# Image/text attention: tasks of each turn and of the first preparation from a written table, turned queries copied by ACT and DVE

## The reference, cut to what matters

```python
q = rms_norm(linear(x, q_w, q_b), norm_q_w).reshape(B, L, NH, HD)
k = rms_norm(linear(ctx_txt, k_w, k_b), norm_k_w).reshape(B, -1, NH, HD)       # 1344 text rows
v = linear(ctx_txt, v_w, v_b).reshape(B, -1, NH, HD)
k_img = rms_norm(linear(ctx_img, k_img_w, k_img_b), norm_k_img_w)...           # 257 image rows
v_img = linear(ctx_img, v_img_w, v_img_b)...
out = (attention(q, k, v) + attention(q, k_img, v_img)).reshape(B, L, DIM)     # two softmaxes
x = x + linear(out, o_w, o_b)                                                  # x was layer-normed first
```

## Time and profile before

| what | us |
|---|---|
| runs, median of 3 | 4134.57 (4131.62 to 4142.93) |
| profiled execution | 4128.62, span 4126.9 |
| PE busy in the span | 3621.0 (88%) |
| DVE busy | 2364.4 (57%) |
| ACT busy | 2263.6 (55%) |
| POOL busy | 784.5 (19%) |

### The profile page before, as it was taken

The page is one execution under the profiler, slowest core; times in us unless marked ns, Lnnn a source line. Parts: engine busy times, 40 slices in busy tenths (PEclk is TensorE's granted clock), DMA queues, the critical chain, the costliest instruction groups (busy, mean ns, idle before and its releaser), DMA issues. The chain is left out here.

```text
span 4126.9 us, 64041 instructions
## 1 busy us (share of the span) xinstructions
PE 3621.0 (88%) x23965; PEld 3060.3 (74%) x23965; DVE 2364.4 (57%) x4251; ACT 2263.6 (55%) x5239; POOL 784.5 (19%) x1026
## 2 busy tenths in 40 slices
PE   6756948999999999995888888785999999999977
PEld 5646937888888888885555555474899999998866
DVE  8964746676676676654555555333455555555445
ACT  3314735676666666663455555412666666666622
POOL 0002123222222222211021020001323232222100
PEclk7767978999999999997899999787999999999989
DMA  4114520010010010001000000112010010100001
GB/s 143 64 39 176 204 97 24 19 46 26 19 51 21 19 51 22 9 6 67 33 18 16 33 1 1 41 66 89 22 53 19 27 53 24 53 24 11 11 31 36
DMA packets 54028, 181.93 MB, mean 44 GB/s; under 512 B 5916, under 2 KB 27872, under 8 KB 46304
## 3 DMA queue, kind: packets, MB, share of 16 engines
q1 hardware_dynamic: 47872, 140.50, 9.9%
q0 software_dynamic: 3696, 35.72, 2.4%
q10 hardware_dynamic: 2160, 1.71, 0.1%
HBM read 149.57 MB, written 24.13 MB: 42 GB/s over the span
## 5 line engine op out<-in xcount | busy, mean ns | idle before, releaser
L1038 PE MATMUL ps<-a_v_rows,a_probs 128*128 128x129 f32 (+1 forms) x7168 | 944.5, 276 | 0.0
L1038 PEld LDWEIGHTS ps<-a_v_rows,a_probs 128*128 128x128 f32 (+1 forms) x7168 | 896.2, 192 | 39.8 <-issue 4.2
L1121 ACT ACTIVATE a_probs<-ps 128x512 f32<-128x512 f32 (+1 forms) x896 | 535.7, 598 | 606.7 <-PE ps L1027 605.9
L1316 DVE TENSOR_REDUCE a_neg<-ps 128x1 f32<-128x1024 f32 (+2 forms) x512 | 540.0, 1056 | 402.2 <-PE ps L1002 401.7
L1131 ACT ACTIVATE ps<-a_negb 128x512 f32<-128x512 f32 (+1 forms) x892 | 536.7, 602 | 58.2 <-DVE a_negb L1331 30.2
L1188 POOL TENSOR_SCALAR a_diag<-ident,a_negmax 128x128 fp32r<-128x128 f32 x256 | 158.1, 618 | 1483.1 <-DVE a_negmax L1324 1481.6
L1023 PE MATMUL ps<-a_qt,a_kt 128*128 128x512 f32 (+1 forms) x896 | 428.7, 478 | 1.4 <-PEq L72 1.4
L2871 ACT ACTIVATE a_probs<-ps 128x1024 f32<-128x1024 f32 x224 | 229.4, 1026 | 277.3 <-PE ps L2744 276.6
L929 PE MATMUL ps<-a_wr,a_ct 128*128 128x256 f32 (+1 forms) x2496 | 362.9, 287 | 9.8 <-DVE a_k_rows L1235 7.7
L929 PEld LDWEIGHTS ps<-a_wr,a_ct 128*128 128x128 f32 (+1 forms) x2496 | 335.9, 187 | 37.3 <-DVE a_k_rows L1235 9.9
L1027 PE MATMUL ps<-a_qt,a_kt 128*128 128x512 f32 (+1 forms) x896 | 355.4, 397 | 0.0
(11 more groups left out here) (393 smaller groups left out, 6151.3 us busy)
## 6 DMA issues: line engine op xcount, KB each, us to landing
a_ct<-ctx_hi SPq DMA_DIRECT2D x12, 1602.0 KB, 6.6
a_ct<-ctx_lo SPq DMA_DIRECT2D x12, 1602.0 KB, 10.4
a_wf<-in_a_wq SPq DMA_DIRECT2D x32, 512.0 KB, 3.5
a_wf<-in_a_wo SPq DMA_DIRECT2D x32, 512.0 KB, 3.6
f_wf<-in_f_experts SPq DMA_DIRECT2D x11, 1088.0 KB, 5.0
a_wf<-in_a_wkv SPq DMA_DIRECT2D x32, 256.0 KB, 2.6
f_u_wf<-in_f_units SPq DMA_DIRECT2D x17, 384.0 KB, 3.0
ctx_hi<-a_ct SPq DMA_DIRECT2D x4, 1602.0 KB, 5.2
```

The costliest lines, as they stand in the source:

```text
L1038: ins = pe.matmul(m.ps[:, 6 + i // 2, (i % 2) * 256:(i % 2) * 256 + VW], probs[0:r, n % 3, i * P:(i + 1) * P], v_rows[g % 2][0:r, t, :], s ...
L1121: act.activation(probs[0:r, n % 3, :], m.ps[0:r, 4 + n % 2, :], ACT.Exp)\
L1316: ins = dve.tensor_reduce(neg2[:, j, r % 2:r % 2 + 1], flat2(m.ps[:, rough_at(task):rough_at(task) + 2, :])[:, 0:e - a0], AX.X, ALU.max, n ...
```

## The change

The row "all" and the rows by group become four full tables, one for each group number mod 4, in which every task has its turn and its place within it. `take_sums` becomes a task TS with a place in the table. The orders of the first preparation are rewritten. Of the two halves of a turned query (QX and QB) ACT copies the first and DVE the second. DVE's QP waits for `qs_lo` and its KP for `kl_done`, since the table could now put them close to the readers of the rows that they overwrite.

```diff
...
 QUAD_TURNS = {
-    "all": (
-        "QX0 KX0 KX1", "KX2 R0 R1 R2", "OX0 KX3 R3 R4", "KX4 R5 R6 R7", "KX5 R8 R9 R10", "KX6 R11 R12 R13",
-        "R14 R15 R16 KH0", "R17 R18 R19 KL0 KH1", "R20 R21 R22 KL1", "R23 R24 R25", "R26 R27 R28", "R29 R30 R31 QS0",
-        "QB0 QL0", ""),
-    0: ("VP12", "VP13", "", "", "", "OR0 OL0", "", "", "Y0", "Y1", "", "", "", ""),
-    1: ("", "", "", "", "NS0", "", "NZ0", "", "KP0 NX0 NL0", "KP1 SQ0", "KP2 SQ1", "KP3 SQ2 KN0", "KP4 SQ3",
-        "KP5 SQ4"),
-    2: ("KP6 SQ5", "KP7 SQ6 KN1", "QP0 KP8 SQ7", "QP1 KP9 SQ8", "KP10 SQ9 QQ0", "KP11 SQ10 KN2 QQ1 QN0", "KP12 SQ11",
-        "KP13 SQ12", "SQ13 KN3", "KH0", "KL0", "XB0", "KH1", "KL1"),
-    3: ("", "", "VP0", "VP1", "VP2", "VP3", "VP4", "VP5", "VP6", "VP7", "VP8", "VP9", "VP10", "VP11"),
+    0: (
+        "QX0 KX0 KX1", "TS0 VP12 KX2 R0 R1", "R2 R3 R4", "R5 R6 VP13 KX3 OX0", "R7 R8 R9",
+        "R10 R11 KX4 R12 KX5 R13 KX6 KH0 R14 R15 R16", "R17 R18 KL0 OL0 QS0 OR0", "KH1 R19 R20", "Y0 R21 R22",
+        "R23 R24 R25", "R26 R27", "R28 R29 R30 KL1", "R31", "Y1 QB0 QL0",
+    ),
+    1: (
+        "KX0 KX1 TS0 QX0", "OX0 KX2 QS0 R0 R1 NS0", "R2 R3 KX3", "R4 R5 R6 KX4 R7 R8 R9 R10", "R11 QL0 R12",
+        "R13 R14", "R15 R16 KX5 KN0 KX6 NZ0 KH0 R17 R18", "R19", "KL0 R20 R21 KH1 R22", "R23 KP0 NX0 R24 NL0 R25",
+        "R26 KL1 KP1 R27 R28 SQ0", "KP2 R29 SQ1", "SQ2 R30 R31 KP3", "QB0 KP4 SQ3 KP5 SQ4",
+    ),
+    2: (
+        "KX0 KX1 QP0", "TS0 QX0 KX2 QP1 KP6 R0 KX3 R1 R2 KX4 R3 KX5 R4 R5 SQ5", "SQ6 KN1 R6 R7 R8",
+        "R9 SQ7 R10 QQ0 KP7 KP8 KP9 R11 OX0 KN2", "R12 SQ8 R13 R14", "R15 KP10 KP11 R16 SQ9 QN0 SQ10", "R17 KX6 R18",
+        "R19 R20 SQ11", "KP12 R21 SQ12 R22 QQ1 R23 KH0", "KN3 KP13 R24 R25 R26 SQ13", "R27 R28 XB0",
+        "R29 R30 R31 QS0", "QL0 QB0 KL0 KL1 KH1", "",
+    ),
+    3: (
+        "QX0 KX0 KX1 TS0", "OX0 KX2", "R0 R1", "R2 R3 VP0 KX3 R4 R5", "R6 R7 R8",
+        "R9 R10 VP1 KX4 KX5 R11 VP2 R12 KX6 VP3 R13 VP4 R14", "R15", "KH0 R16 R17 R18", "R19 R20 KH1 KL0",
+        "R21 VP5 R22", "R23 R24", "KL1 R25 R26", "QS0 R27 VP6 R28 VP7 R29 QL0", "R30 R31 VP8 VP9 QB0 VP10 VP11",
+    ),
 }
 QUAD_FIRST = (
-    "NS0 KP0 KP1 W2 NZ0 KP2 SQ0 SQ1 NX0 SQ2 KN0 KP3 KP4 NL0 SQ3 KP5 SQ4 KP6 SQ5 SQ6 KN1 ND0 QP0 QP1 QQ0 QQ1 QN0 KP7 KP8 "
-    "SQ7 W3 KP9 SQ8 KP10 SQ9 SQ10 KN2 ND1 KP11 QS0 KP12 SQ11 QL0 KP13 SQ12 SQ13 KN3 QX0 ND2 KH0 VP0 VP1 KL0 VP2 KX0 KX1 "
-    "R0 R1 R2 R3 R4 R5 R6 R7 KX2 KX3 VP3 ND3 KH1 VP4 VP5 KL1 VP6 KX4 KX5 KX6 R8 R9 R10 R11 R12 R13 R14 R15 VP7 R16 R17 "
-    "R18 R19 R20 R21 R22 R23 VP8 VP9 R24 R25 R26 R27 R28 R29 R30 R31 VP10 VP11 QB0"
+    "NS0 KP0 NZ0 KP1 W2 KP2 NL0 SQ0 NX0 KN0 W3 KP3 SQ1 SQ2 KP4 QP0 QP1 QQ0 SQ3 SQ4 KN1 KP5 KP6 ND0 SQ5 KP7 KP8 "
+    "QN0 SQ6 QQ1 SQ7 SQ8 SQ9 KP9 ND1 KP10 KP11 KN2 SQ10 VP0 VP1 KP12 QL0 SQ11 QS0 SQ12 ND2 KP13 KH0 KL0 SQ13 VP2 "
+    "KN3 QX0 ND3 KX0 KX1 VP3 R0 R1 VP4 R2 KH1 VP5 R3 R4 R5 KL1 KX2 KX3 R6 R7 R8 VP6 R9 R10 R11 VP7 R12 R13 R14 "
+    "KX4 R15 R16 R17 R18 KX5 R19 R20 R21 R22 KX6 R23 R24 R25 R26 R27 R28 VP8 R29 R30 R31 VP9 QB0 VP10 VP11"
 )
-QUAD_SECOND = "VP12 VP13 QS0 QL0 KH0 KL0 KH1 KL1"
+QUAD_SECOND = "KL0 QS0 KH0 KH1 VP12 QL0 KL1 VP13"
 QUADS = 4
...
             to, last = g + 2 if g >= 0 else 0, QUAD_GROUPS
-        elif kind == "OX":
+        elif kind in ("TS", "OX"):
             to, last = g - 1, QUAD_GROUPS
...
     for g in range(QUAD_GROUPS):
-        own = QUAD_TURNS[g % QUADS]
-        for t in range(turns):
-            names = QUAD_TURNS["all"][t]
-            if g % QUADS == 2:
-                names = " ".join(n for n in names.split() if n[:2] not in ("KH", "KL"))
-            plan.append(quad_tasks(names + " " + own[t], g))
+        plan += [quad_tasks(QUAD_TURNS[g % QUADS][t], g) for t in range(turns)]
     first = quad_tasks(QUAD_FIRST, -1)
     second = [(kind, 0 if kind == "VP" else 1, i) for kind, _to, i in quad_tasks(QUAD_SECOND, -1)]
-    last = quad_tasks("OX0", QUAD_GROUPS) + quad_tasks("OR0 OL0 Y0 Y1", QUAD_GROUPS)
+    last = quad_tasks("TS0 OX0", QUAD_GROUPS) + quad_tasks("OR0 OL0 Y0 Y1", QUAD_GROUPS)
     return first + second, plan, last
...
     number = {task: k for k, task in enumerate(slots)}
-    nth = {}
+    nth, of_kind = {}, {}
     for task in flat:
-        nth[task] = 1 + sum(1 for other in nth if other[0] == task[0])
+        of_kind[task[0]] = nth[task] = of_kind.get(task[0], 0) + 1

...

+        def turned_queries(h, bank, i):
+
+            rows = slice(STK * i, STK * (i + 1))
+            return qt[h % 2][rows, :, i * S:(i + 1) * S], bank[rows, :].rearrange("p (h n) -> p h n", n=S)
+
         def staged(k):
...

-                def take_queries(h, bank, done):
-                    for i in range(2):
-                        rows = slice(STK * i, STK * (i + 1))
-                        act.activation(qt[h % 2][rows, :, i * S:(i + 1) * S],
-                                       bank[rows, :].rearrange("p (h n) -> p h n", n=S), ACT.Copy).then_inc(done, 1)
-
                 def QX(h, i):
                     act.wait_ge(qx_ready, nth[("QX", h, i)])
-                    take_queries(h, slot(("QX", h, i)), qx_done)
+                    act.activation(*turned_queries(h, slot(("QX", h, i)), 0), ACT.Copy).then_inc(qx_done, 1)

...
                     act.wait_ge(qb_ready, nth[("QB", h, i)])
-                    take_queries(h, slot(("QB", h, i)), qb_done)
+                    act.activation(*turned_queries(h, slot(("QB", h, i)), 0), ACT.Copy).then_inc(qb_done, 1)

...
                         dve.wait_ge(qs_hi, QUADS * b)
+                        dve.wait_ge(qs_lo, QUADS * b)
                     dve.tensor_tensor(q_rows[:, q, :], slot(("QP", b, q))[:, 0:D], qo_bias[:, 0, :], ALU.add)\
...
                     dve.wait_ge(kp_ready, nth[("KP", b, t)])
+                    if b:
+                        dve.wait_ge(kl_done, nth[("KL", QUADS * b - 1, 1 if t >= SPLIT[1] else 0)])
                     dve.tensor_tensor(k_rows[0:r, t, :], slot(("KP", b, t))[0:r, 0:D], kv_bias[0:r, g, 0:D], ALU.add)\
...
                                       q_st[h % 2][:, :, :, 0:HDS].bitcast(F32), ALU.subtract).then_inc(qs_lo, 1)
+
+                def QX(h, i):
+                    dve.wait_ge(qx_ready, nth[("QX", h, i)])
+                    dve.tensor_copy(*turned_queries(h, slot(("QX", h, i)), 1)).then_inc(qx_done, 1)
+
+                def QB(h, i):
+                    dve.wait_ge(qb_ready, nth[("QB", h, i)])
+                    dve.tensor_copy(*turned_queries(h, slot(("QB", h, i)), 1)).then_inc(qb_done, 1)

...

-                def take_sums(g):
+                def TS(g, _i):
                     dve.wait_ge(pv_done, KT * (g + 1))
...
                 does = {"W": W, "NS": NS, "NZ": NZ, "NL": NL, "QP": QP, "KP": KP, "VP": VP, "ND": ND, "KL": KL, "QL": QL, "R": R,
-                        "OX": OX, "OL": OL, "Y": Y}
+                        "QX": QX, "QB": QB, "TS": TS, "OX": OX, "OL": OL, "Y": Y}
                 dve.memset(m.ps[:, ACC, :], 0.0).then_inc(ot_zero, 1)
...
                         does[kind](to, i)
-                for n, turn in enumerate(turns):
-                    g, t = divmod(n, KT)
-                    if g and t == 1:
-                        take_sums(g - 1)
+                for turn in turns:
                     for kind, to, i in turn:
...
                             does[kind](to, i)
-                take_sums(QUAD_GROUPS - 1)
                 for kind, to, i in behind:
```

## The result

The changed kernel takes 3993.2 us (median of 4, 3989.97 to 3999.47) against 4134.5 before: ratio .9657, 95% interval .9638 to .9675. The profiled execution took 3994.06, its span 3992.3.

What follows compares the result with a forecast made beforehand. TensorE was busiest (88%), with 172 us of waits and low clock in the attention loop. 4128.6 - (659 - 559) for the loop - 3 for the preparation = 4025.6, plus 6 for the median: 4032 us, range 3995 to 4094.

Steps and rivals of the forecast that it cites:

- The clock step: Attention loop: of 119 us at PE's low clock, half (60) stays, each losing .45, adding 27 us.
- The waits: Attention loop: 3 us of waits on average in each of 15 groups with preparation, 45 us in all.
- The walk: New table traced turn by turn with assumed handover times: group 0 takes 31.5 us, 1.9 above its load.
- the load of 487: Whole attention loop: PE's tasks at full clock without waits sum to 487 us, against 659 measured.
- Rival (a): Attention loop: the walk is right as it is and the clock hardly falls; loop 531, time 4004 us; chance .17.
- POOL at the end of group 2: QN and KN3 finish near group 2's end, where ACT's KH1 and PE's next QX wait; group +3.7 us.
- Queries by two engines: Turned-query copies: ACT loses 2 x .59 us a group, DVE gains as much; worth -.5 to +1 a group.
- that sign: Turned-query copy: DVE's half of QX starts within .3 us of ACT's if the forecast is right.
- Preparation: First preparation, 54.8 us before the loop: reordered lists save 3 us, bounds -3 to +9.
- Rival (b): Tightly filled turns: ACT and DVE alternate, waits shrink by a third only, clock stays; 55 saved, 4080 us; chance .22.
- (c): Attention loop: no change, since waits come from the ring of three slots in every order; 4130 +- 12; chance .07.
- (d): Slower: PE's clock stays low through turns with one R or none and into the next group; 4161 us; chance .06.

Runs made afterwards that it cites:

- tables_act: Changed kernel with both halves of every turned query copied by ACT again, orders as changed: 4008.4 us, ratio .9704.
- old_prep: Changed kernel with the two task lists of the first preparation as they were before: 4000.3 us, ratio .9677.
- after_again: The changed kernel unchanged, run again beside others on one chip: 3997.0 us, ratio .9674 to the kernel before.
- split_kx_last: Kernel before with turned queries copied by ACT and DVE, and KX behind the R in turns 1 to 5: 4063.6 us, ratio .9838.
- kx_thrice: Kernel before with PE doing the four transposes of each KX three times: 4109.9 us, ratio .9951.
- old_row_1: Changed kernel with the old row of tasks in groups 1, 5, 9 and 13 alone: 4023.7 us, ratio .9736.
- kx_last: Kernel before with KX behind the turn's R instead of ahead in turns 1 to 5: 4100.2 us, ratio .9922.

## Why the forecast fell outside its range, step by step

- *The clock step failed.* "With PE waits of .2 to .5 instead of .8 to 1 I take half, 60 us; [...] That adds 27". In the changed kernel, tables_act and old_prep the loop's clock reads 1.00, so the 27 us are 0 to 3 (the repeat, after_again, has 6.8 us at the lower level, at .45 each). I had halved a quantity that answers in another way: split_kx_last got it back (.99) with 69 us of idle time left, and kx_thrice (1.00) with 43. The full clock was there before the waits were gone, so no share of them should have been carried over. Nor does the clock follow the sum of the waits: old_row_1 reads .97 with 29 us of idle time, split_kx_last .99 with 69. Where the waits lie counts; what exactly brings the clock down, these runs leave open.
- *The waits were over-hedged.* The walk gave 31.5 us for group 0; 31.7 was measured. For groups 1 to 3 it gave 33.4, 38.0 and 38.0; 34.1, 37.2 and 36.4 were measured. I then raised its mean of 2.3 a group to 3. The loop is 36.6 above the load of 487 instead of 45: 8.4 us too many. Not all of the 36.6 are waits: PE is idle for 15.7 of them, and its busy time at the full clock, 507.9, is 21 above my load. So the hedge was partly right for another reason, a load reckoned too small. Rival (a), 531 for the loop, was nearest, and it had .17. With the clock at 0 and the walk's mean my own sum gives 487 + 34 = 521 for the loop and 3994, just below the range, whose lower end stopped at (a) with some room. That this meets the measured 3993.2 so closely is partly luck: the loop came 2.6 us above 521, and the errors outside it, below, took that back.
- *POOL at the end of group 2* holds nobody up: no engine waits for KN or QN there. What group 6 loses above its load, 2.9 us, lies half in its turn 1 (6.7 us from one exponential to the next, for a load of 5.3) and .8 at QB (2.2 for 1.4).
- *Queries by two engines.* The estimate (inside the walk, up to 1 us a group) fits the 9.8 us of tables_act. In the old table the same edit took 33 us off the loop, through the clock. DVE's copy of 64 partitions takes .695, as long as that of 128 in the earlier trace rows. The halves can overlap whole, as in the QB of group 0, at the end of the preparation:

```profile
1973.07 0.70 DVE L3046 CAST a_qt<-ps 64x512 fp32r<-64x512 f32 x1 [0.30 <-PE ps L2695]
1973.07 0.59 ACT L2863 ACTIVATE a_qt<-ps 64x512 fp32r<-64x512 f32 x1 [6.26 <-PE ps L2695]
```

  By the rule of the Trainium skill ("PSUM — Partial Sum Buffer", PSUM bank collisions) that two engines may use different quadrants of one bank at once, this was to be expected, and the trace agrees. DVE's half starts with ACT's here, but .6 us ahead of it in the QX of group 6, where ACT is at its exponential, and is then nearly done before ACT's begins; that sign was badly chosen.
- *TS, the new waits, VP13*: next to nothing, as costed. PE waits 1.2 us in the whole loop for TS's copy, and never for a load.
- *Preparation*: 4.6 us for 3.
- *The rest.* 6.0 us were lost outside (above), and the median after lies .9 below its profiled execution while that before lies 6 above. 27 + 8.4 + 1.6 - 6.0 + 6.8 = 37.8 of the 38.8 us between forecast and median; the last 1 is rounding of these windows.
- Rival (b) fell: turn by turn loads add up to 140 a batch, and the batch takes 139.4. (c) fell with PE's idle time, 88.0 to 15.7 us with the same ring of three; (d) with the clock at 1.00, also in the turns with one R.

## What to carry to other kernels

Where a busy engine's clock falls in the profile, compare its busy time for the same instructions with what they take at the full rate: here that was half of the gain, and it came back whole, not in proportion to the waits removed. A result in a ring slot whose copy stands behind long work of another engine should have tasks of other engines between it and the next user of that slot. When a walk through the queues with the trace's own durations gives a number, forecast that number and put the doubt into the range.

## What the runs showed of the hardware that I had not expected

DVE's addition into `o_rows` (128 columns, both operands in SBUF) takes .29 us alone, and 1.30 or 1.48 when POOL's long products run beside it; in the rows below it ends .14 us after POOL's instruction. Its mean over the 16 groups is .516 us after (three of them at 1.48 to 1.50), against .313 before (one at .63). The case of kx_last, group 6, shows the price: the reduction behind it comes late, PE waits 1.07 us for that slot, and the same six products that take .94 a turn later take 1.25, as the clock falls (.71 from 2238.4 to 2239.8, .50 from there to 2242).

```profile
2236.05 1.90 POOL L2910 TENSOR_TENSOR a_k_rows<-a_k_rows,a_sq 128x1024 f32<-128x1024 f32 x1
2236.79 1.30 DVE L3060 TENSOR_TENSOR a_o_rows<-a_o_n 128x128 f32<-128x128 f32 x1
2238.02 0.75 DVE L3038 TENSOR_REDUCE a_q_st<-ps 128x1 fp32r<-128x257 f32 x2
2238.49 1.25 PE L2643 MATMUL ps<-a_wr,a_zt 128*128 128x256 f32 x6 [1.07 <-DVE a_q_st L3038]
...
2243.96 0.94 PE L2643 MATMUL ps<-a_wr,a_zt 128*128 128x256 f32 x6
```

In the changed kernel the same happens beside KN1 in group 6 (1.48 us), and PE does not wait behind it:

```profile
2192.57 2.39 POOL L2916 TENSOR_TENSOR a_k_rows<-a_k_rows,a_norm_w 128x1024 f32<-128x1024 f32 x1
2193.62 1.48 DVE L3076 TENSOR_TENSOR a_o_rows<-a_o_n 128x128 f32<-128x128 f32 x1
```

That the two engines exclude each other is read from the times alone; no run tested it.
